# Second products of a mixture of experts on high and low parts, and first weights fetched per tile

## The reference

```python
logits = jnp.einsum('sbd,de->sbe', x, Wg) + bg + bias
vals, idx = jax.lax.top_k(logits, TOP_K)          # 2 of 16 experts per token
w = jax.nn.softmax(vals - jnp.max(vals, axis=-1, keepdims=True), axis=-1)
cw = jnp.einsum('sbk,sbke->sbe', w, jax.nn.one_hot(idx, NUM_EXPERTS, dtype=x.dtype))
h = jax.nn.relu(jnp.einsum('sbd,edh->esbh', x, W1) + b1[:, None, None, :])
y = jnp.einsum('esbh,ehd->esbd', h, W2) + b2[:, None, None, :]
out = jnp.einsum('esbd,sbe->sbd', y, cw)
```

## Time and profile before

| | us |
|---|---|
| median of 3 runs | 1706.76 |
| the three runs | 1708.32, 1706.76, 1703.58 |
| the profiled execution | 1704.07 (span 1702.4) |
| granted PE clock, mean | 0.924 |

### The profile page before, as it was taken

How to read it: one execution, slowest core, us unless ns; L and a number is a source line. 1 busy time by engine, 2 the same in 40 slices (tenths; PEclk the granted TensorE clock), 3 DMA queues, 4 the chain that set the end, 5 groups by cost and what they waited for, 6 DMA issues and landing times. The chain is left out here.

```text
span 1702.4 us, 40120 instructions
## 1 busy us (share of the span) xinstructions
PE 1510.4 (89%) x14095; PEld 991.9 (58%) x14097; DVE 1180.6 (69%) x2263; ACT 983.3 (58%) x2029; POOL 429.4 (25%) x702
## 2 busy tenths in 40 slices
PE   6999999999999999998999857999774599999990
PEld 5843333333333333336788846888662299999980
DVE  7689999999999999934888676454568722222225
ACT  3428888888888888881555413443221055555543
POOL 3045401101010101001022236222121145555540
PEclk9968999999999999999999958998786599999995
DMA  6950232333232323012000012332129422222218
GB/s 216 294 158 16 46 62 48 63 54 68 50 60 52 66 46 59 9 22 34 1 1 0 1 41 76 100 103 61 45 64 335 152 73 71 70 71 68 71 59 296
DMA packets 123206, 135.24 MB, mean 79 GB/s; under 512 B 29540, under 2 KB 94072, under 8 KB 122936
## 3 DMA queue, kind: packets, MB, share of 16 engines
q1 hardware_dynamic: 110296, 107.60, 24.9%
q0 software_dynamic: 7584, 20.72, 3.7%
q10 hardware_dynamic: 5184, 4.98, 0.9%
HBM read 92.23 MB, written 36.04 MB: 75 GB/s over the span
## 5 line engine op out<-in xcount | busy, mean ns | idle before, releaser
L1985 DVE TENSOR_REDUCE mx<-ps 128x1 f32<-128x1024 f32 x512 | 622.8, 1221 | 21.9 <-PE ps L2134 16.4
L2023 ACT ACTIVATE PR<-ps 128x512 f32<-128x512 f32 x1024 | 557.1, 599 | 84.3 <-PE ps L2188 34.6
L2134 PE MATMUL ps<-KQ 48*128 48x512 f32 x1024 | 388.4, 461 | 3.2 <-DVE mx L1985 2.8
L2188 PE MATMUL ps<-KQ 50*128 50x512 f32 x1024 | 378.0, 449 | 0.2
L2170 PE MATMUL ps<-PR,VO 128*32 128x256 f32 x4096 | 328.9, 393 | 9.1 <-ACT PR L2023 8.6
L2188 PEld LDWEIGHTS ps<-KQ 50*128 50x128 f32 x1024 | 154.5, 186 | 216.0 <-ACT PR L2023 198.4
L2170 PEld LDWEIGHTS ps<-PR,VO 128*32 128x32 f32 x4096 | 80.7, 108 | 195.2 <-ACT PR L2023 99.3
L2134 PEld LDWEIGHTS ps<-KQ 48*128 48x128 f32 x1024 | 158.4, 191 | 21.2 <-DVE mx L1985 20.5
L1877 PEld LDWEIGHTS ps<-e_xinT,e_w 128*128 128x128 f32 x1264 | 156.6, 195 | 5.8 <-issue 1.8
L1877 PE MATMUL ps<-e_xinT,e_w 128*128 128x128 f32 x1264 | 157.5, 279 | 1.1 <-ACT e_xinT L1809 1.1
L1867 PE MATMUL ps<-eW,e_hiddenT 128*128 x632 | 149.6, 380 | 0.0
(11 more groups left out here) (283 smaller groups left out, 2178.9 us busy)
## 6 DMA issues: line engine op xcount, KB each, us to landing
qk_parts<-parts SPq DMA_DIRECT2D x8, 2048.0 KB, 8.4
TB<-toeplitz_lines SPq DMA_DIRECT2D x32, 512.0 KB, 6.4
KQ<-qk_parts SPq DMA_DIRECT2D x96, 128.0 KB, 4.6
KQ<-qk_parts SPq DMA_DIRECT2D x192, 64.0 KB, 2.4
eW<-in_L_ffn_W SPq DMA_DIRECT2D x16, 512.0 KB, 6.5
eW<-in_L_ffn_W SPq DMA_DIRECT2D x8, 1024.0 KB, 12.5
e_got<-expert_outputs SPq DMA_DIRECT2D x16, 512.0 KB, 9.3
X<-in_L_attn_x SPq DMA_DIRECT2D x8, 512.0 KB, 4.3
```

The source lines that it names most:

```text
L1985: nc.vector.tensor_reduce(mx[:, u % RING, h * QT + q:h * QT + q + 1], ps[:, b:b + 2].rearrange("p a n -> p (a n)"), AX, ALU.max, negate=Tr ...
L2023: nc.scalar.activation(PR[:, kt % 2, h], ps[:, st_bank(u, s)], ACT.Exp).then_inc(exp_done, 1)
L2134: made = nc.tensor.matmul(ps[:, max_bank(u, t) + k], of_tile(queries(u % RING), h, q), kq[half(h, KROWS), 0, h % HR, k * BANK:(k + 1) * BA ...
L2188: nc.tensor.matmul(ps[:, st_bank(u, s)], kq[half(h, AROWS), 0, h % HR, kt * P:(kt + 1) * P], queries(u % RING)[half(h, AROWS), qc, h % HR] ...
```

## The change

Two things in moe, nothing elsewhere.

The second product is no longer a float32 matmul of hT by W2. The hidden tile and the tile's second weights are each split into a high part (a float32r copy, by ACT) and a low part (the difference, by DVE), and the product is three float32r products: high by high, low by high, high by low. So ACT copies 128 x 1024 of W2 per tile (second_weights, in the place of first_weights) and in addition 128 x 512 of the hidden tile (end of half); DVE subtracts 128 x 1024 (start of body) and 128 x 512 (low, end of body); PE does twelve float32r matmuls of 128 x 128 by 256 per tile in the place of four float32 ones.

The first weights are no longer kept for all experts. In stage 2 SP reads the owner of tile k and loads its first weights (512 KB) from memory into one of four buffers, as soon as the first products of tile k - 4 are done; PE reads that buffer. In stage 1 the sixteen loads of W1 are gone, and W2's eight loads of 1 MB take their place, one behind the store of each chunk. b2b is now loaded behind the first weights of tile 1.

```diff
--- before.py
+++ after.py
@@ -1466,14 +1466,13 @@
 
     y_rows = nc.dram_tensor("expert_outputs", [FREE * P + 2 * T, D], F32, kind="Internal").ap()
     with ExitStack() as st:
-        W1 = sbuf(st, "eW1", [P, E, DK, EH])
         W2 = sbuf(st, "eW2", [P, E, EK, D])
         b1T = sbuf(st, "b1T", [P, E * EK])
         weight = sbuf(st, "weight", [P, 2, NT])
         owner = sbuf(st, "owner", [P, MT], I32)
         token = sbuf(st, "token", [P, MT], I32)
         y_row = sbuf(st, "y_row", [P, MT], I32)
-        w_loaded = [sem(f"e_w_loaded{q}") for q in range(2)]
+        w2_loaded = sem("e_w2_loaded")
 
         with ExitStack() as s0:
             xc = sbuf(s0, "e_xn", [P, 2, CT, D])
@@ -1533,18 +1532,11 @@
                     for h in range(2):
                         sp.sem_inc(stored[h], 16)
 
-                    def first_weights(e):
-                        sp.dma_start(W1[:, e], w1_in[e].rearrange("(k p) h -> p k h", p=P)).then_inc(w_loaded[0], 16)
                     for c in range(NC):
                         sp.wait_ge(norm.ready, c + 1)
                         sp.dma_start(xrows[CW * c:CW * (c + 1)].rearrange("(k p) d -> p k d", p=P), xc[:, c % 2]).then_inc(stored[c % 2], 16)
-                        first_weights(c)
-
-                    for e in range(NC, E):
-                        first_weights(e)
-                    for q in range(NC):
-                        es = slice(q * E // NC, (q + 1) * E // NC)
-                        sp.dma_start(W2[:, es], w2_in[es].rearrange("e (k p) d -> p e k d", p=P)).then_inc(w_loaded[1], 16)
+                        es = slice(c * E // NC, (c + 1) * E // NC)
+                        sp.dma_start(W2[:, es], w2_in[es].rearrange("e (k p) d -> p e k d", p=P)).then_inc(w2_loaded, 16)
                     for h in range(2):
                         sp.wait_ge(stored[h], 16 * (NC // 2 + 1))
 
@@ -1749,14 +1741,19 @@
             AHEAD = 4
             xin = sbuf(s1, "e_xin", [P, AHEAD, D])
             xT = sbuf(s1, "e_xinT", [P, 2, DK, P])
-            w1 = sbuf(s1, "e_w1", [P, 2, DK, EH])
+            w1 = sbuf(s1, "e_w1", [P, AHEAD, DK, EH])
             hT = sbuf(s1, "e_hiddenT", [P, 2, EK, P])
+            h_split = [sbuf(s1, f"e_hidden{a}", [P, 2, EK, P], F32R) for a in range(2)]
+            w2_split = [sbuf(s1, f"e_w2_{a}", [P, 2, EK, D], F32R) for a in range(2)]
             y = sbuf(s1, "e_y", [P, 2, D])
             b2b = sbuf(s1, "b2b", [P, E, D])
             x_loaded = [sem(f"e_x_loaded{r}") for r in range(AHEAD)]
             stored = [sem(f"e_y_stored{z}") for z in range(2)]
-            b2_loaded, w1_kept, xt_done, xt_kept, ht_done, hta_kept, htb_kept, m2_done, y_kept = (
-                sem("e_" + n) for n in ("b2_loaded", "w1_kept", "xt_done", "xt_kept", "ht_done", "hta_kept", "htb_kept", "m2_done", "y_kept"))
+            w1_loaded = [sem(f"e_w1_loaded{r}") for r in range(AHEAD)]
+            b2_loaded, xt_done, xt_kept, ht_done, hta_kept, htb_kept, h_high, h_low, w2_high, w2_low, m2_done, y_kept = (
+                sem("e_" + n) for n in ("b2_loaded", "xt_done", "xt_kept", "ht_done", "hta_kept", "htb_kept", "h_high", "h_low", "w2_high", "w2_low", "m2_done", "y_kept"))
+            flat = lambda v: v.rearrange("p k n -> p (k n)")
+            w2_of = lambda e: W2[:, ds(e, 1)].rearrange("p a k d -> p (a k d)")
             assert AHEAD % 2 == 0
             FIRST = AHEAD + 1
             XT_BANK, HA_BANK, HB_BANK, Y_BANK = (0, 7), (1, 2), (3, 4), (5, 6)
@@ -1776,8 +1773,14 @@
             with nc.Block() as block:
                 @block.sync
                 def _(sp):
-                    sp.wait_ge(x_loaded[1], 16)
-                    sp.dma_start(b2b[:], b2_in.partition_broadcast(P)).then_inc(b2_loaded, 16)
+                    for k in range(MT):
+                        r = k % AHEAD
+                        if k >= AHEAD:
+                            sp.wait_ge(ht_done, k - AHEAD + 1)
+                        e = of_tile(sp, k)
+                        sp.dma_start(w1[:, r], w1_in[ds(e, 1)].rearrange("a (k p) h -> p (a k) h", p=P)).then_inc(w1_loaded[r], 16)
+                        if k == 1:
+                            sp.dma_start(b2b[:], b2_in.partition_broadcast(P)).then_inc(b2_loaded, 16)
 
                 @block.gpsimd
                 def _(pool):
@@ -1809,20 +1812,26 @@
                         nc.scalar.copy(xT[:, z].rearrange("p k n -> p (k n)"), ps[:, XT_BANK[z], 0:D]).then_inc(xt_kept, 1)
                         if not is_first(k):
                             half(k - 1, 1 - z)
-                        if not (isinstance(k, int) and k == MT - 1):
-                            first_weights(k + 1, 1 - z)
-
-                    def first_weights(k, z):
+                        second_weights(k, z)
+
+                    def second_weights(k, z):
                         e = of_tile(act, k)
-                        nc.scalar.copy(w1[:, z].rearrange("p k h -> p (k h)"), W1[:, ds(e, 1)].rearrange("p a k h -> p (a k h)")).then_inc(w1_kept, 1)
+                        if not isinstance(k, int) or k >= 2:
+                            act.wait_ge(m2_done, k - 1)
+                        nc.scalar.copy(w2_split[0][:, z].rearrange("p k d -> p (k d)"), w2_of(e)).then_inc(w2_high, 1)
 
                     def half(k, z):
                         e = of_tile(act, k)
                         act.wait_ge(ht_done, k + 1)
+                        if not isinstance(k, int) or k >= 2:
+                            act.wait_ge(h_low, k - 1)
+                            act.wait_ge(m2_done, k - 1)
                         for j in range(HK):
                             nc.scalar.activation(hT[:, z, j], ps[:, HA_BANK[z], j * P:(j + 1) * P], ACT.Relu, bias=b1T[:, ds(EK * e + j, 1)]).then_inc(hta_kept, 1)
-                    act.wait_ge(w_loaded[0], 16 * E)
-                    first_weights(0, 0)
+                        act.wait_ge(hta_kept, HK * (k + 1))
+                        act.wait_ge(htb_kept, HK * (k + 1))
+                        nc.scalar.copy(flat(h_split[0][:, z]), flat(hT[:, z])).then_inc(h_high, 1)
+                    act.wait_ge(w2_loaded, 16 * NC)
                     tiles(act, body)
                     half(MT - 1, (MT - 1) % 2)
 
@@ -1836,16 +1845,25 @@
                             dve.wait_ge(stored[z], 16 * (k // 2))
                         nc.vector.tensor_tensor(y[:, z], ps[:, Y_BANK[z], 0:D], b2b[:, ds(e, 1), :].rearrange("p a d -> p (a d)"), op=ALU.add).then_inc(y_kept, 1)
 
+                    def low(k, z):
+                        dve.wait_ge(h_high, k + 1)
+                        nc.vector.tensor_tensor(flat(h_split[1][:, z]), flat(hT[:, z]), flat(h_split[0][:, z]).bitcast(F32), op=ALU.subtract).then_inc(h_low, 1)
+
                     def body(k, r):
                         z = r % 2
                         e = of_tile(dve, k)
+                        dve.wait_ge(w2_high, k + 1)
+                        nc.vector.tensor_tensor(flat(w2_split[1][:, z]), w2_of(e), flat(w2_split[0][:, z]).bitcast(F32), op=ALU.subtract).then_inc(w2_low, 1)
                         dve.wait_ge(ht_done, k + 1)
+                        if not isinstance(k, int) or k >= 2:
+                            dve.wait_ge(h_low, k - 1)
                         for j in range(HK, EK):
                             nc.vector.tensor_scalar(hT[:, z, j], ps[:, HB_BANK[z], (j - HK) * P:(j - HK + 1) * P], b1T[:, ds(EK * e + j, 1)], 0.0, ALU.add, ALU.max).then_inc(htb_kept, 1)
                         if is_first(k):
                             dve.wait_ge(b2_loaded, 16)
                         else:
                             outputs(k - 1, r - 1)
+                        low(k, z)
                     tiles(dve, body)
                     outputs(MT - 1, MT - 1)
 
@@ -1859,22 +1877,22 @@
                         last.then_inc(xt_done, 1)
 
                     def second(k, z):
-                        e = of_tile(pe, k)
                         pe.wait_ge(y_kept, k + 1)
-                        pe.wait_ge(hta_kept, HK * (k + 1))
-                        pe.wait_ge(htb_kept, HK * (k + 1))
-                        for j in range(EK):
-                            last = nc.tensor.matmul(ps[:, Y_BANK[z], 0:D], hT[:, z, j], W2[:, ds(e, 1), j, :].rearrange("p a d -> p (a d)"), start=(j == 0), stop=(j == EK - 1))
+                        pe.wait_ge(w2_low, k + 1)
+                        pe.wait_ge(h_low, k + 1)
+                        todo = [(a[:, z, j], w[:, z, j]) for j in range(EK) for a, w in split_products(h_split, w2_split)]
+                        for n, (a, w) in enumerate(todo):
+                            last = nc.tensor.matmul(ps[:, Y_BANK[z], 0:D], a, w, start=(n == 0), stop=(n == len(todo) - 1))
                         last.then_inc(m2_done, 1)
 
                     def body(k, r):
                         z = r % 2
-                        pe.wait_ge(w1_kept, k + 1)
```

(4 more changed lines are left out.)

## The result

| | before | after |
|---|---|---|
| median, us | 1705.17 (1701.22 to 1708.32, 4 runs) | 1725.53 (1723.68 to 1730.9, 4 runs) |
| profiled execution, us | 1704.07 (span 1702.4) | 1724.12 (span 1722.4) |
| mean granted PE clock | 0.924 | 0.919 |

The ratio is 1.0113, 95% interval 1.0084 to 1.0142: slower by 0.8 to 1.4%. The forecast was 1712.2 us, or +0.3%, so the direction was right and the size too small: the median lies in the stated range of 1696 to 1743, but above the 1706 to 1719 that were given the highest chance.

What follows compares the result with a forecast made beforehand. A loop of waits between ACT and DVE, 3.77 us a tile, was to bound stage 2. Stage 2 +3.4 and stage 1 +2 made +5.4, 1709.5 on the profiled execution; 2.7 more for the median gave 1712.2, range 1696 to 1743.

Steps and rivals of the forecast that it cites:

- the circle: Stage 2 loop of waits, ACT's W2 high, DVE's W2 low and ReLUs, ACT's hidden high: 3.77 us a looped tile.
- PE's need, 3.57: PE's work per stage 2 tile: 1.46 for twelve products plus 2.11 for first products and transposes, 0.16 us less than before.
- Stage 2 from end to end, +3.4: Stage 2 was to end at 1659.3 in the place of 1655.9, most of the +3.4 us in the tail.
- the forecast's own three pieces: Stage 2: start until W2 low of tile 2 at 1368.3, 285.9 us to W2 low of tile 78, then 5.1 us.
- it just fits: Start of stage 2: b2b's 2 MB load, 6 us, fits within the first two tiles at half clock, costing 0 to 2 us.
- The tail, 5.1: End of stage 2: from W2 low of tile 78 to the end of its second products, 5.1 us.
- I price the clock at nothing: Stage 2: PE, busy 3.57 of 3.77 us, was to keep the full granted clock, at no cost.
- Stage 1, +2 within 0 to 3.5: Stage 1: 1.05 MB behind each store delays the store that the last norm waits for, 2 us, up to 3.5.
- The weights from memory, nothing in the loop: Stage 2: first weights loaded per tile, 208 GB/s with gathers and scatters, cost nothing while three tiles of lead hold.
- PE sets the pace: Rival for stage 2: expert read hidden under ACT's 0.62 copy, loop 3.57 us a tile, 1697 us in all; chance 0.20.
- DVE and POOL exclude each other: Rival for stage 2: POOL's indirect DMAs hold W2 low 0.3 to 0.6 us, 34 us more, 1746 in all; chance 0.13.
- a longer circle: Rival for stage 2: hidden waits add 0.15 us a tile, 11 us, 1723 in all; chance 0.12 including late weights.

Runs made afterwards that it cites:

- the ReLUs first: Changed kernel with DVE's ReLUs moved ahead of W2's low part: 1689.76 us, ratio 0.9896 on chip A; again on chip C 1700.25 us, 0.9969.
- W2 behind the last store: Changed kernel with DVE's ReLUs ahead of W2 low and all W2 loads after the eighth store: 1694.15 us, ratio 0.9924; with b2b moved, 1690.95 to 1696.4 us.
- the second part alone: Kernel before with first weights loaded per tile and W2 loaded behind the stores, second products still float32: 1709.96 us, ratio 1.0021 on chip A.
- one read fewer: Changed kernel with ACT's W2 high always copying expert 0's weights, so no expert read there: 1702.95 us, ratio 0.9975 on chip B.

## Why the prediction was right or wrong

- *PE would not set the pace; the circle would.* Right, and shown by cutting it. Steps as named: W2 high 1.05 (1.04 forecast); to DVE 0.15 (0.15); W2 low 1.14 to the next start (1.13); ReLUs 0.60 and 0.03 (0.61 and 0.04); hidden high to W2 high 0.82 (0.80). Sum 3.79 against 3.77. Two links taken from quite different places held to 0.02. One term was missing: once in four tiles, as the loop turns, DVE starts 0.26 to 0.28 after ACT's end instead of 0.15, and that tile takes 3.90.
- *PE's need, 3.57.* Wrong in size: 3.45. Both of its terms were too high: twelve products took 1.42, not 1.46, and "first products and transposes 2.11" became 2.02. The work in the second term did not change. By the starts of the matmuls, the first products up to the transposes take 1.79 in both kernels (here 1504.95 to 1506.74; with the ReLUs first, above, 1505.52 to 1507.31), and the old second products 1.73, not 1.62:

```profile
1503.22 1.89 PE L1867 MATMUL ps<-eW,e_hiddenT 128*128 x8
1504.95 1.95 PE L1877 MATMUL ps<-e_xinT,e_w 128*128 128x128 f32 x16
1506.74 0.38 PE L1858 MATMUL ps<-ident,e_xin 128*128 128x128 f32 x2
1506.95 1.89 PE L1867 MATMUL ps<-eW,e_hiddenT 128*128 x8
```

Behind the old second products the next weight load starts 0.21 before its matmul (1504.74 and 1504.95), ahead of them 0.10 (1503.12 and 1503.22), so the cut at loads had booked 0.1 of the second products under what stays. PE's read of the tile's expert (line 1764), which the change removes, is not the cause: in the kernel before PE's sequencer does it from 1504.97 to 1505.69, while the first products run, and these take the same 1.79 without it. The error did not show in the result, since the ring stood over it, but it sets what the repair is worth: 0.37 a tile instead of 0.20.

- *Stage 2 from end to end, +3.4.* Measured +9.5 (1.3 + 8.2). By the forecast's own three pieces, from the sorted tiles at 1360.0: W2 low of tile 2 was to start 18.0 later and started 19.3 later, at 1379.27 (+1.3); from there to W2 low of tile 78, 289.7 for 285.9 (+3.8, of which 18 turns of 0.11 are 2.0, the rest the 0.02 a tile and tiles with constant numbers of 3.68 for 3.62); the tail +1.0. The first piece is there before any product of tile 0: the first gather is issued 1.55 after the sort in both kernels, but PE's first transposes, which wait for it, start 5.9 after the sort and not 4.7; in every kernel that fetches first weights per tile they start 5.8 to 6.1 after it (7.1 in one), with b2b loaded beside or not. That the weights' loads slow the gather is argued, not shown. b2b is waited for, where I had said that it just fits: DVE's first low 3.11 us, and PE 1.01 more. But this wait is not shown to cost anything: with the ReLUs first, the first second products start 15.8 to 16.0 after the sort with b2b loaded here, and 15.8 with it loaded in stage 1.

```profile
1374.81 0.69 DVE L1850 TENSOR_TENSOR e_hidden<-e_hiddenT,e_hidden 128x512 fp32r<-128x512 f32 x1 [3.11 <-DMA b2b<-in_L_ffn_b]
1375.64 1.66 PE L1885 MATMUL ps<-e_w,e_hidden 128*128 128x256 f32 x12 [1.01 <-DVE e_hidden L1850]
```

- *The tail, 5.1.* Measured 6.1: from W2 low at 1669.01 to 1675.13. The last twelve products came at a lower pace after PE's idle 2 us, 2.52 for the weight loads against 1.49. The granted clock was 1.00 up to 1672 and 0.50 from 1673 to the end of the products, the lower of PE's two levels, 1.2 GHz. So the step that failed here is "I price the clock at nothing": it held in the loop and not in the tail, where "twelve products and the drain 1.6" measured 2.8:

```profile
1669.01 1.23 DVE L1856 TENSOR_TENSOR e_w<-eW,e_w 128x1024 fp32r<-128x1024 f32 x1 [0.50 <-ACT e_w L1821]
...
1672.31 2.52 PEld L1885 LDWEIGHTS ps<-e_w,e_hidden 128*128 128x128 f32 x12 [2.19 <-issue]
1672.34 2.79 PE L1885 MATMUL ps<-e_w,e_hidden 128*128 128x256 f32 x12 [2.01 <-DVE e_hidden L1850]
```

- *Stage 1, +2 within 0 to 3.5.* The mechanism was right and the size under, beyond its upper bound: +3.8 here, 27.6 and 27.5 in the changed kernel's two traces, against 23.8. By the semaphore events of the trace the first six stores land 3.4, 4.7, 5.3, 5.8, 7.1 and 7.5 us after their issue, the 0.8 a chunk that was forecast. But I let only the last norm wait, and the last two do: the spaces before the last two stores grew by 1.5 and 2.2. In the rows, which answer to the earlier trace rows, DVE waits 0.37 for a store, then 1.89, which the profile lays to POOL; the store issued at 1287.52 lands at 1294.67, 0.39 before that norm starts, so it is the store. SP took 1.75 to issue W2's sixth piece where the five before took 0.51. The four traces with W2 behind the last store have 23.8:

```profile
1289.85 1.38 DVE L95 TENSOR_SCALAR e_xn<-X,ln_mv,ln_rstd 128x256 f32 x4 [0.37 <-DMA expert_inputs<-e_xn]
1291.25 0.37 SPq L1537 DMA_DIRECT2D expert_inputs<-e_xn  x1
1291.66 1.75 SPq L1539 DMA_DIRECT2D eW<-in_L_ffn_W  x1
1295.06 1.38 DVE L95 TENSOR_SCALAR e_xn<-X,ln_mv,ln_rstd 128x256 f32 x4 [1.89 <-POOL ln_rstd L88]
```

- *The weights from memory, nothing in the loop.* Right, shown by the second part alone: PE busy 260.00 of 260 us.
- *Rival, PE sets the pace.* Fell: the expert's read is not hidden under the hidden copy (0.82, and 0.52 without it).
- *Rival, DVE and POOL exclude each other.* Fell in its price: DVE's W2 low takes 1.21 to 1.24, with eight of 869 at 1.25 to 1.29. The exclusion exists the other way round (below).
- *Rival, a longer circle, 1723.* Its total, 1723, is near the first comparison's 1725.5, but its mechanism is not what happened: the circle is 0.05 a tile longer than forecast and not 0.15, and half of what the loop lost over the forecast sits in its turn (2.0 of 3.8) and not in the waits named; that the total fits is luck. The forecast's circle was right and its sum 7.9 us short (13.3 for 5.4): 3.8 in the loop, 1.8 in stage 1, 1.3 at the start of stage 2, 1.0 in the tail.

## What to carry to other kernels

When work is moved off the bounding engine, sum the rings and not only the engines: list each engine's program order and its waits, and look for a closed path through one tile. Here three instructions in another order turned +0.7% into -1.0% on one chip; on another the reordered kernel had -0.3%. Before reordering to cut a ring, walk the buffers too, since a wait for a free slot is an edge like any other; and put large loads behind the small store that a chain waits for, not between.

## What the hardware showed unexpectedly

**An indirect DMA that starts inside a DVE subtraction of two SBUF inputs ends about 0.85 us after it.** In the changed kernel's first trace:

```profile
1501.47 1.23 DVE L1856 TENSOR_TENSOR e_w<-eW,e_w 128x1024 fp32r<-128x1024 f32 x1 [0.78 <-ACT e_w L1821]
...
1501.87 1.68 POOL L1791 DMA_INDIRECT e_xin<-expert_inputs,token  x1 [0.30 <-issue]
```

and in its second, where POOL happened to start first:

```profile
1503.37 0.97 POOL L1791 DMA_INDIRECT e_xin<-expert_inputs,token  x1 [0.30 <-issue]
1503.51 1.23 DVE L1856 TENSOR_TENSOR e_w<-eW,e_w 128x1024 fp32r<-128x1024 f32 x1 [0.67 <-ACT e_w L1821]
```

POOL takes 1.68 or 0.97, DVE 1.23 both times, and both stretches are 307.4 to 307.5 us: here POOL had the slack. From 1400 to 1620 us all 51 indirect DMAs of the first trace that start inside W2 low take 1.55 to 1.88 and end 0.84 to 0.85 after it; in the second, 114 of 115 start outside such a subtraction and take 0.97 to 0.99. Inside DVE's ReLUs, whose input lies in PSUM, they are not held: 54 in the trace before take 0.97 to 0.98. Where POOL starts only 0.01 to 0.04 after the subtraction, it can be the one that goes ahead: five times in the first trace it keeps 0.99 and hidden low takes 0.73 to 0.77 in the place of 0.69.

**The same kernel has two tile rates.** With the ReLUs first, 279.1 us on chip A and 287.5 on chip C, instruction for instruction the same. It is not one stray execution: the four runs on A took 1684.92 to 1691.39 us, the twelve on C 1697.41 to 1708.36, with the kernel before at 1706.22 and 1704.91. The slower trace differs once in each turn of the four-tile loop, 16 times and 7.6 us in all from 1400 to 1620:

```profile
DVE e_y L1846 <- PE ps L1885: 7.6, 16, 0.5
```

One such turn:

```profile
1513.13 0.61 DVE L1859 TENSOR_SCALAR e_hiddenT<-ps,b1T 128x128 f32<-128x128 f32 x2 [0.73 <-PE ps L1895]
1513.66 1.22 DVE L1861 TENSOR_TENSOR e_w<-eW,e_w 128x1024 fp32r<-128x1024 f32 x1
1515.34 0.42 DVE L1846 TENSOR_TENSOR e_y<-ps,b2b 128x256 f32<-128x256 f32 x1 [0.46 <-PE ps L1885]
```

against, in the faster trace:

```profile
1521.83 0.61 DVE L1859 TENSOR_SCALAR e_hiddenT<-ps,b1T 128x128 f32<-128x128 f32 x2 [0.73 <-PE ps L1895]
1522.36 1.22 DVE L1861 TENSOR_TENSOR e_w<-eW,e_w 128x1024 fp32r<-128x1024 f32 x1
1523.51 0.42 DVE L1846 TENSOR_TENSOR e_y<-ps,b2b 128x256 f32<-128x256 f32 x1
```

The profile lays the gap to PE, and its semaphore events agree. The twelve products that DVE wants start at 1512.56; at their usual spacing they end at 1514.23, before DVE is free at 1514.88. But the semaphore that the last of them raises, m2_done, is raised at 1515.03, 0.80 later, and DVE starts behind that. In the faster trace it is raised 0.02 after the end. From 1400 to 1620 this signal comes 0.77 to 0.94 late once in each turn in all four slower traces, and never over 0.02 late in the two faster ones; in the run with one read fewer, on chip B, it is 0.41 to 0.45 late once in each turn. The first products behind it start on time. Since the ends of matmuls are modelled in the profile, the trace does not tell whether the last product or only its signal is late, and what makes it so stays open. For the comparison it means that a gain of 8 us in this loop may or may not be had, by chip as far as three chips show: the repair alone is worth 1.0% on A and 0.3% on C; with W2 late, and b2 moved too in three of four cases, it is 0.8 to 1.0% on all three.
